# Loads moved to another queue and preparation reordered in a four-layer residual kernel on one core

## The reference

```python
x = x + L0(x, types)      # scores = tanh(x @ W1 + b1) . v; masked softmax over the sequence; weighted mean of x / count
x = x + L1(x, ...)        # 16-head attention, head size 8; per sequence either a sparse softmax over 32 given
                          # indices or a dense one with a bias of strength lam = 10 * exp(-5 * u)
x = x + L2(x, ids8)       # h = relu(x Wi' + 2 x A Ci' + expert low-rank(x)); out = h Wo' + 2 h A Co' + expert low-rank(h)
x = x + L3(x, ids16)      # h = gelu(x fc1' + b); out = [h fc2' + b | h experts_w[id]' + experts_b[id]]
```

## Time and profile before

| What | Value |
|---|---|
| median of 3 runs | 304.65 us (304.23 to 306.5) |
| the profiled execution | 309.48 us, span in the trace 307.7 us |
| TensorE matmuls busy | 246.9 us, 80% of the span |
| VectorE busy | 202.5 us, 66% |
| ScalarE busy | 133.1 us, 43% |
| GpSimd busy | 117.2 us, 38% |
| moved by DMA | 48.77 MB, 159 GB/s over the span |

### The profile page before, as it was taken

The page is one execution under the profiler, slowest core; times in us unless marked ns, Lnnn a source line. Parts: engine busy times, 40 slices in busy tenths (PEclk is TensorE's granted clock), DMA queues, the critical chain, the costliest instruction groups (busy, mean ns, idle before and its releaser), DMA issues.

```text
span 307.7 us, 13475 instructions
## 1 busy us (share of the span) xinstructions
PE 246.9 (80%) x5226; PEld 183.8 (60%) x5226; DVE 202.5 (66%) x387; ACT 133.1 (43%) x225; POOL 117.2 (38%) x224
## 2 busy tenths in 40 slices
PE   0189676501918997999999999999999998999875
PEld 0166333200616865777786678678777876767855
DVE  2539599700339798659968995987799698642031
ACT  2044724100315284429455743845384375516121
POOL 4883253100046645412633353254426325411350
PEclk9999999755578999999999999999999999999979
DMA  7233225778920377436736672774577477067401
GB/s 234 120 82 125 70 71 143 195 221 257 295 55 2 77 232 223 129 102 213 215 123 192 211 239 75 209 230 141 164 211 215 148 236 223 37 177 239 137 36 36
DMA packets 36097, 48.77 MB, mean 159 GB/s; under 512 B 11345, under 2 KB 16209, under 8 KB 35938
## 3 DMA queue, kind: packets, MB, share of 16 engines
q1 hardware_dynamic: 35600, 47.95, 51.9%
q10 hardware_dynamic: 466, 0.39, 0.4%
HBM read 44.14 MB, written 4.19 MB: 157 GB/s over the span
## 4 chain that ended last, share of the span: by engine, by line
PE 58%; DVE 11%; issue 10%; SPq 9%; DMA 7%; ACT 2%; POOL 1%; ACTq 1%; POOLq 0%; DVEq 0%
PE pB L787 8%; PE pB L820 7%; PE pB L742 6%; PE pB L738 5%; PE pB L739 5%; SPq L280 5%; SPq L281 4%; PE pX L713 4%; DMA rank_s<-rank_w_dram 4%; PE pV L728 3%; PE pV L700 3%; DVE sc L1126 3%; PE pX L680 3%; PE pX L738 2%; PE pV L734 2%
## 5 line engine op out<-in xcount | busy, mean ns | idle before, releaser
L401 POOL TENSOR_TENSOR sc<-sc,rmax 128x512 f32<-128x512 f32 x32 | 33.5, 1049 | 87.5 <-DVE rmax L1129 55.6
L427 POOL COPY rw<-e3t_s 128x128 f32 x128 | 39.9, 313 | 52.3 <-issue 42.0
L1126 DVE SCALAR_TENSOR_TENSOR sc<-pX,bias 128x512 f32<-128x512 f32 x32 | 21.7, 679 | 21.7 <-PE pX L713 21.4
L527 ACT ACTIVATE ex<-sc 128x512 f32<-128x512 f32 x32 | 20.1, 629 | 35.5 <-POOL sc L401 35.5
L820 PE MATMUL pB<-rw,hT 128*32 128x128 f32 x960 | 32.5, 275 | 0.6 <-ACT hT L535 0.4
L1135 DVE STREAM_TRANSPOSE pt<-ex 128x512 f32<-128x512 f32 x32 | 22.3, 698 | 9.9 <-ACT ex L527 9.9
L820 PEld LDWEIGHTS pB<-rw,hT 128*32 128x32 f32 x960 | 24.7, 109 | 6.1 <-issue 6.1
L787 PE MATMUL pB<-rw,hT 128*32 128x128 f32 x896 | 27.4, 274 | 0.0
L713 PE MATMUL pX<-kb,qs 32*32 32x128 f32 x1024 | 17.5, 296 | 11.6 <-DVE sc L1126 10.9
L1119 DVE TENSOR_SCALAR kb<-pX,bqk,cols_s 128x512 f32<-128x512 f32 x32 | 24.2, 800 | 1.6 <-PE pX L742 1.6
L531 ACT ACTIVATE hT<-pB 128x512 f32<-128x512 f32 x28 | 16.6, 597 | 18.7 <-PE pB L742 18.7
(11 more groups left out here) (199 smaller groups left out, 532.1 us busy)
## 6 DMA issues: line engine op xcount, KB each, us to landing
rw<-w_d SPq DMA_DIRECT2D x128, 256.0 KB, 3.0
rw<-fc2t_dram SPq DMA_DIRECT2D x4, 768.0 KB, 7.6
xN<-xn_dram SPq DMA_DIRECT2D x8, 256.0 KB, 2.7
w_d<-rw SPq DMA_DIRECT2D x4, 512.0 KB, 3.2
xT<-xt_dram SPq DMA_DIRECT2D x7, 256.0 KB, 2.8
out_dram<-o_s SPq DMA_DIRECT2D x7, 256.0 KB, 2.7
e3t_s<-e3t_dram SPq DMA_DIRECT2D x1, 1024.0 KB, 6.1
ffn_s<-ffn_w_dram SPq DMA_DIRECT2D x1, 896.0 KB, 11.6
```

Of the source, the lines that this page charges most:

```text
L401: pool.tensor_tensor(sc[:, g % 2, :, :], sc[:, g % 2, :, :], rmax[:, g % 2, :].unsqueeze(2).to_broadcast([P, H, S]), ALU.subtract).then_in ...
L427: pool.tensor_copy(rw[:, r, :, SHARED:D], e3t_s[:, bass.ds(e, 1), :, :].rearrange("p o c n -> p (o c) n"))\
L1126: stt(sc[:, g % 2, :, :], score_cols, SCALE, bias[:, bass.ds(t, 1), :].to_broadcast([P, H, S]), ALU.mult, ALU.add).then_inc(sc_sb, 1)
```

## The change

Four groups of edits. (1) SyncE's queue: xT(0) comes first; the loads of x for blocks 1 and 2 go, and so do the fc2t loads from behind the sixteen fetches: they are issued right behind e3t, which no longer has a waiting load ahead of it. (2) ScalarE's queue: xT(0) leaves; rank_s is loaded as 16 full rows and one row of 128 columns; xN(1), xT(1) are issued by ScalarE ahead of expert_wo(0), and xN(2), xT(2) ahead of its queries(1); a tanh of one column stands ahead of all computation, on a column which GpSimd clears first. (3) Order: TensorE does shared_part(0), shared_part(1) ahead of values(0), ScalarE expert_wo(0), expert_wo(1) ahead of its values(0); TensorE's prepare_biases comes ahead of scores(0, 0), its scorer_in(2) in step 1 behind scores(1, 0); GpSimd makes the ids before the strength and its first weight_lows after subtract_max(0, 2). (4) VectorE makes the bias of blocks 0 and 1 in one go (256 columns instead of twice 128), and the masks and counts of blocks 1 and 2 ahead of x1(0).

```diff
@@ sync
+            sp.dma_start(xT[:, :], xt[0]).then_inc(ld_xT, 16)
             sp.dma_start(ints_s[:, :], ints).then_inc(ld_ints, 16)
...
-            load_xN(1)
-            load_xT(1)
             sp.dma_start(e3t_s[:, :, :, :], e3t).then_inc(ld_rw, 16)
+            for c in range(FC):
+                sp.dma_start(rw[:, :, c, 0:SHARED],
+                             fc2t[:, c, :].unsqueeze(1).to_broadcast([P, ROWS, SHARED])).then_inc(ld_rw, 16)
             for c in range(FC):
                 sp.wait_ge(w2_sb, 2 * c + 2)
...
-            load_xN(2)
             sp.wait_ge(ids_sb, 1)
             sp.wait_ge(st_w2, 16 * FC)
             for g in range(G):
                 expert_weights2(0, g)
-            load_xT(2)
-            for c in range(FC):
-                sp.dma_start(rw[:, :, c, 0:SHARED],
-                             fc2t[:, c, :].unsqueeze(1).to_broadcast([P, ROWS, SHARED])).then_inc(ld_rw, 16)
@@ gpsimd
+            pool.memset(spare[:, :], 0.0).then_inc(spare_sb, 1)
...
+            prepare_ids()
             prepare_strength()
-            prepare_ids()
...
             subtract_max(0, 1)
-            weight_lows(0, H_FC1, 1, 0)
             pool.wait_ge(prep, P_BO)
             biased_x1(0)
             subtract_max(0, 2)
+            weight_lows(0, H_FC1, 1, 0)
@@ scalar
-            act.dma_start(xT[:, :], xt[0]).then_inc(ld_xT, 16)
...
-            act.dma_start(rank_s[:, :], rank_w).then_inc(ld_rank, 16)
+            act.dma_start(rank_s[0:E3, :], rank_w[0:E3, :]).then_inc(ld_rank, 16)
+            act.dma_start(rank_s[E3:E3 + 1, R_FB:R_END], rank_w[E3:E3 + 1, R_FB:R_END]).then_inc(ld_rank, 16)
+            act.wait_ge(spare_sb, 1)
+            act.activation(spare[:, :], spare[:, :], ACT.Tanh).then_inc(spare_sb, 1)
+
+            def load_x(i):
+                act.wait_ge(pool_ps, i)
+                act.dma_start(xN[:, :, :], xn[i]).then_inc(ld_xN, 16)
+                act.wait_ge(x1_sb, i)
+                act.dma_start(xT[:, :], xt[i]).then_inc(ld_xT, 16)
...
+            load_x(1)
+            expert_wo(0)
+            expert_wo(1)
             act.wait_ge(prep_pool, 1 + Q4)
             values(0)
-            expert_wo(0)
-            expert_wo(1)
...
             expert_wo(7)
+            load_x(2)
             queries(1)
@@ tensor
-            pe.wait_ge(ld_rank, 16)
+            pe.wait_ge(ld_rank, 32)
...
+            shared_part(0)
+            shared_part(1)
             pe.wait_ge(ld_attn, 16)
             values(0)
-            shared_part(0)
-            shared_part(1)
+            prepare_biases()
             scores(0, 0)
-            prepare_biases()
...
                 low(n - 1)
-                if next_block:
+                if next_block and last is not None:
                     scorer_in(n + 1)
                 values(n)
                 scores(n, 0)
+                if last is None:
+                    scorer_in(n + 1)
@@ vector
-                for args in bias_steps(0, G):
+                for args in bias_steps(0, 2 * G):
...
             prepare_hits()
+            mask_tokens(G, 3 * G)
+            count_tokens(G, 3 * G)
             x1(0)
...
-            mask_tokens(G, 3 * G)
...
-            second_bias()
...
-            count_tokens(G, 3 * G)
```

More of the change, by code:

```diff
@@ L199, in cond_resid_kernel @@
         woh_sb, wol_sb = sem("woh_sb"), sem("wol_sb")
-        pprep = sem("pprep")
+        pprep, spare_sb = sem("pprep"), sem("spare_sb")
         bias_sb = sem("bias_sb")
@@ L564, in product @@
                 act.activation(temp[:, :], ps[:, :], ACT.Copy, scale=ALPHA).then_inc(tmp_sb, 1)
+            act.wait_ge(spare_sb, 2)
             act.wait_ge(ld_b1v, 32)
@@ L1071, in prepare_biases @@
                 assert PREP_VEC[0] == P_BO
-            def second_bias():
-                for args in bias_steps(G, 2 * G):
-                    step(tt(*args))
             def pool_weights(i, part):
@@ L1277 @@
 P_MK = 5
[L1278 to L1282, removed]
+P_COUNT = 18
+P_BIAS = 23
+P_BO = 25
+Q_IDS = 9
+Q_STRENGTH = 14
 L0_STEPS = 8
```

## The result

The changed kernel takes 277.92 us (median of 4 runs, 276.38 to 281.25) against 305.57 for the kernel before in the same measurement (304.23 to 307.17): ratio 0.9076, 95% interval 0.8997 to 0.9156; the medians differ by 27.7 us. Ratios leave out executions over 1.5% longer than the fastest of their kernel (here the one of 281.25 us), medians don't. The forecast was 275.2, range 270.5 to 280.5. The profiled execution takes 276.38 us, span 274.5, which is 33.1 us less than the profiled one of before (309.48), where 29.4 were forecast. In the rows the start and the length come first, in us.

The account below looks back on a forecast made before the run. TensorE bounds the untouched loop, so gains come before step 2: 17.7 - 0.6 + 5.5 + 6.8 (preparation: 3.5 + 1.1 + 2.2) = 29.4 us; 304.65 - 29.4 = 275.2 us, range 270.5 to 280.5.

Parts of the forecast that it names:

- 17.7 us of xT(2): Step 1: issuing x of block 2 from ScalarE removes TensorE's wait behind sixteen fetches, so first scores come 17.7 us earlier.
- 0.6 us for scorer_in(2): Step 1: scorer_in(2) behind scores(1, 0) delays ScalarE's tanh and values, so the exponential starts later, costing 0.6 us.
- fc2t, 5.5 us less 0.6: Step 1: early fc2t loads free GpSimd's first subtraction; 5.5 us gained, limited by TensorE's scores(1, 2); 0.6 is scorer_in(2)'s cost.
- the 6.9 of the other bound: Step 1: GpSimd's first subtract_max started 6.9 us late, held by fc2t loads; at most that is gained.
- the rival of a warm TensorE: Step 1: without its stall TensorE may keep full clock, gaining 2.0 and 1.4 us more: 272; chance 0.13.
- rank_s: Start: two loads land it sooner, ending TensorE's wait; keys(0) then wait for GpSimd, 3.5 us gained.
- Halves ahead of values: Preparation: two matrix halves ahead of values(0) let its copy lie beside TensorE's next halves; scores(0, 1) gain 1.1 us.
- VectorE's list: Preparation up to x1(1): mask (0.87) and second bias (0.73 and twice 0.29) leave VectorE's chain, gaining 2.2 us.
- l0s subtraction: Preparation: VectorE's 1.57 us subtraction ran beside GpSimd's weight_lows, which moves; up to 1.3 us more, outside the sum.
- the mask's new place: Ahead of x1(0): the mask may lengthen GpSimd's list of ids by up to 0.9 us, where keys(0) wait.
- The fetches: Rival: out2(0, 0) would wait for fetched weights, the last landing near 75; costs 1 to 2 us: 276.7, chance 0.05.
- the rival with 0.01: Loop: TensorE's clock falls to half and stays, each such pass costing up to 27 us more; chance 0.01.

Follow-up runs that it names:

- after_again: The changed kernel itself measured once more, beside three variants on one chip: 278.12 us, ratio 0.9019 to the kernel before.
- b_x2_act: The kernel before with only xN(2) and xT(2) moved from SyncE to ScalarE, ahead of queries(1): 307.09 us, ratio 0.9991.
- a_fc2t_late: The changed kernel with the four fc2t loads back behind the fetches of block 0: 300.59 us, ratio 0.9839 to the kernel before.
- a_values_first: The changed kernel with values(0) ahead of the two matrix halves again, on TensorE and ScalarE: 278.83 us, ratio 0.9110 to the kernel before.
- a_vector_old: The changed kernel with VectorE's mask, counts and second bias back between the groups of block 0: 281.76 us, ratio 0.9163 to the kernel before.
- v_pool_order: The changed kernel with attention weights' low part early in GpSimd's list and ScalarE copying wo's high part ahead of queries(0): 276.80 us, ratio 0.8980.
- a_rank_whole: The changed kernel with rank_s in one load of 17 rows: 280.49 us, ratio 0.9103 to the kernel before.
- b_fc2t_early: The kernel before with only the four fc2t loads moved, issued early instead of behind the sixteen fetches: 302.17 us, ratio 0.9863.
- v2_pool_order: As v_pool_order, but with the strength's short operations ahead of GpSimd's long spread of the factors: 276.33 us, ratio 0.9010.

## Why the prediction was right, step by step

**The 17.7 us of xT(2)** are right, as a step in this order: from x1(1) to the first scores of step 1 took 27.2 us and takes 8.4, 18.7 less. It is one us more than forecast, because TensorE ran keys(1) at full clock, one matmul in 0.23 us instead of 0.43, so VectorE got its keys sooner. ScalarE's two issues cost 0.33 and 0.34 us. The 0.6 us for scorer_in(2) in its new place did not appear: ScalarE was through with its values at 53.95, and its exponential started at 54.42, when GpSimd's subtraction was done.

**fc2t, 5.5 us less 0.6:** from the first scores to out2(0, 0) took 20.45 and takes 13.74, 6.7 less. The bound from TensorE's scores(1, 2) was read at half clock; at full clock they were done at 55.5. So the 6.9 of the other bound came through almost whole up to here, in this execution. With the 9.0 us of the preparation this makes 34.4 at out2(0, 0); its gap of 1.24 leaves the 33.2 by which the spans differ. The part of the rival of a warm TensorE that I gave 0.13 did happen here, if only until 58: then TensorE went on at 0.57 for 4 us. But nothing of it was kept. In *after_again* the clock was at 0.70 from 52 to 56 already, and out2(0, 0) started at 67.09 instead of 65.52; yet its first three groups ended at 69.9 there and at 69.8 here, behind the gap, and x1(2) was read at 71.03 and 70.91. From the first scores to x1(2) took 24.4 us before and 19.1 in both executions of the changed kernel: 5.3 us less, the forecast 5.5. What holds out2 to that moment no row names.

But the way I split the 22.6 us between two edits was an accident of order. I wrote that the fc2t stall "follows at once" and costed it at its own length. *b_x2_act* and *a_fc2t_late* show that fc2t late costs 23.3 us, and that moving xT alone gives nothing that can be told. Both hang on one thing, the 17 to 18 us that SyncE needs to issue sixteen fetches. The sum was safe only since the change makes both edits.

**rank_s:** the mechanism holds; keys(0) wait for GpSimd (3.66 us) as said, 4.7 us earlier instead of 3.5, because GpSimd began its list 1.8 us earlier, b1v having landed sooner, and lost about 0.5 on the way. Of these 4.7 us the first scores kept 3.5 (26.65 instead of 30.19). **Halves ahead of values:** 1.1 forecast, 1.2 in the trace of *a_values_first*. scores(0, 1) come 5.6 us earlier (27.84 instead of 33.44), where 4.6 were forecast. **VectorE's list:** 2.2 forecast; from there to x1(1) the traces of before and after differ by 3.4 us, *a_vector_old* and *after_again* by 3.3. The total is nearer than its terms. The mask's 0.87 was counted as lying on the chain and did not: VectorE waited behind it. The second bias gave 1.4 and the counts, with what stands around them, 0.6. The l0s subtraction, which was left out of the sum as a bound, took 0.29 instead of 1.57 and gave 1.3: so collisions with GpSimd are part of the price of a VectorE instruction in this stretch. Against the mask's new place, 0.9 us had been held possible; *a_vector_old*, which has no mask there, starts keys(0) at 17.73, and the two executions of the changed kernel at 17.65 and 17.76, so it costs nothing that shows. GpSimd's operation of 1.00 instead of 0.74 us above ran beside the cast and the subtraction of x1, not beside the mask. The rule that stood behind it, of the Trainium skill, page "SBUF — State Buffer", section "Who interferes with whom", as the prediction has it for instructions with two inputs, agrees with the slow subtractions (1.64 and 1.65 instead of 0.74, in *v_pool_order* and *a_rank_whole*); the slow casts and the table operations of one input (1.35, 2.02, 1.33) it doesn't cover. All of the preparation: x1(1) comes 9.0 us earlier, not 6.8.

**Why the medians give less than the trace.** 33.1 us by the two profiled executions, 27.7 by the medians. The profiled one of before lies 3.9 us above its median of 305.57, that of after 1.5 below its own. The traces show three places where executions differ.

The first is the preparation: the profiled one of before waited for rank_s until 14.50, and the same single load let TensorE start at 11.82 and 12.33 in the traces of *b_x2_act* and *b_fc2t_early*. x1(0) was read 2.7 and 2.2 us earlier there, x1(1) 1.5 and 0.9 earlier. The second is SyncE's issuing, where I had put the doubt, and rightly: the fetches and fc2t took 27.6 us in before and 26.0 in *b_x2_act*. The third is TensorE's granted clock. The first pass of the loop takes 29.9 us in before and 30.4 in the profile after, both at 1.00, but 31.5 in *after_again*, at 0.95 (the window has TensorE's busy time behind its length, and the clock third from the end):

```profile
79.01:110.50 31.49, 29.06 (x649) 22.05 (x648) 23.18 (x45) 15.25 (x27) 11.29 (x23) 0.95 0.51 154
```

That is nearly all of the 1.7 us between the spans of the two executions of the changed kernel. And the stretch from x1(3) to the end took 171.2 to 171.8 us in the four traces whose last 20 us ran at 1.00, and 172.4 to 174.6 in the ten at 0.91 to 0.98, before (173.5) and after (173.2) among them. How often each of these falls in an unprofiled execution no run here shows, so the 5.4 us are placed only in kind. I predicted too low a median because I took the profiled difference off it unchanged, and because the 304.65 that I took it off is 0.9 below the median of the later measurement; the forecast of 29.4 lies between the two differences.

**The rivals.** The fetches did not become the bound as far as a row shows: they were issued from 46.58 to 63.87, and the row behind the 1.24 us gap in out2(0) names no DMA. ScalarE's issues were cheap. The clock stayed at 1.00 in the loop of the profiled execution. In *after_again* and five other kernels of the fourteen it fell in the first pass, to 0.95 on the mean of the pass, and was back at 1.00 in the next: the mechanism of the rival with 0.01, for a part of one pass and at 1.5 us instead of 27.

## What to carry to other kernels

Where two stalls stand one behind the other in a trace, look what releases each: if both releasers sit behind the same queue, removing the first alone pays nothing, because the second then takes its length. Cost the two together, and say in which order the terms hold. A queue's order is also the order of its issuing time: sixteen computed addresses at 1.1 us each are 18 us for whatever stands behind them, however small. Look also whether the engine waits behind an instruction before you count it as time on the chain: the mask's 0.87 us were followed by 1.30 us of waiting. And give an instruction of VectorE on the critical chain the price that it has beside GpSimd's long ones, not its own.

## What the runs showed that I had not expected

- A load of 17 rows (93.5 KB) held up an 8 KB table issued on the other queue: it landed 8.1 us after its issue instead of 4.2, in the one kernel that issued both at the same time. The 896 KB of FFN weights landed 10.1 to 11.6 us after their issue with it and 6.0 to 7.2 without. Its own landing varied from 9.0 to 11.8 us between executions.
- VectorE operations of 0.18 us took 1.33 and 1.19 beside GpSimd operations of 1.89 and 1.26 us, and a cast of 0.43 us took 2.02 beside the former in *a_rank_whole*. Reordering GpSimd's list moved the collision from one victim to the next, in *v_pool_order* and *v2_pool_order*.
- The first pass of the loop took 29.3 to 32.4 us in fourteen traces, every later one 27.5. Two things make it up. TensorE idles for 2.0 to 3.9 us in it, against 0.5 later, in part with no releaser, for instance in the changed kernel (the rows below). And in six of the traces the granted clock was 0.95 over the pass, with TensorE busy for 28.8 to 29.1 us, against 27.3 to 27.5 in the eight at 1.00.

```profile
86.54 0.43 PE L830 MATMUL pB<-rw,hT 128*32 128x128 f32 x8 [1.17 <-issue]
90.68 0.29 PE L738 MATMUL pV<-vb,pt 128*32 128x36 f32 x10 [1.75 <-issue]
```

- TensorE's granted clock was 0.57 from 58 to 62 us, after 8 us in which the engine had been busy for 5.04, and 1.00 from 62 on. In *after_again*, the same kernel, it was 0.70 from 52 to 56.
